# Ending the first attention layer in a block of its own, beside the next layers' loads and context products

## What is computed

```python
x = x + tanh(g_xattn[0]) * L0_xattn(layernorm(x), ctx)          # 16 heads of 32, context of 128 tokens
x = x + tanh(g_ffn[0])   * L0_ffn(layernorm(x))                 # 256 chosen tokens of each batch
x = x + tanh(g_xattn[1]) * L1_xattn(layernorm(x), ctx)          # 16 heads of 64
x = x + tanh(g_ffn[1])   * L1_ffn(layernorm(x))                 # ternary weights, conv
# L0_ffn:
scores = x @ w_router
_, idx = jax.lax.top_k(scores, 256)          # the tokens that are processed
x_sel = take(x, idx)                         # attention and gated MLP on them alone
out = x.at[idx].set(x_proc)
```

## Time and profile before

| | us |
|---|---|
| median of 3 runs | 1968.17 (1965.85 to 1969.87) |
| time of the profiled execution | 1974.4 |
| its span, first to last instruction | 1972.4 |
| attention slots (DVE's last L868 starts) | 482.06 |
| last gather issued | 536.67 |
| first load of the block that follows | 541.90 |
| first instruction of the second layer (L1812) | 578.83 |

### The profile page before, as it was taken

One profiled execution on the slowest core, in us unless ns is written; L12 is line 12 of the kernel. 1 busy time (PEld: TensorE's weight loads), 2 busy tenths in 40 slices (PEclk: granted clock), 3 DMA queues, 4 the chain that ended last, 5 costly groups with the idle time before them and its releaser, 6 DMA issues. The chain is left out here.

```text
span 1972.4 us, 24959 instructions
## 1 busy us (share of the span) xinstructions
PE 1615.3 (82%) x9331; PEld 934.4 (47%) x9331; DVE 1288.3 (65%) x2061; ACT 810.9 (41%) x1317; POOL 555.0 (28%) x482
## 2 busy tenths in 40 slices
PE   5788988887358879957899998999997267888886
PEld 3444444443143644424566665666664234444443
DVE  3468888888611442324477775777766379999996
ACT  3344444432012623223433432433432057777773
POOL 3222222211211200022221111102200077777771
PEclk9899999999679999977899999999998689999999
DMA  4012222012370233331101102012011230111211
GB/s 168 21 44 86 86 86 86 28 38 85 107 284 22 99 131 112 128 110 61 43 21 55 55 23 75 22 54 76 1 54 32 75 145 6 59 59 59 81 64 43
DMA packets 73124, 142.33 MB, mean 72 GB/s; under 512 B 8257, under 2 KB 17621, under 8 KB 72746
## 3 DMA queue, kind: packets, MB, share of 16 engines
q1 hardware_dynamic: 72042, 137.55, 19.6%
q0 software_dynamic: 960, 3.15, 0.5%
HBM read 97.67 MB, written 43.01 MB: 71 GB/s over the span
## 5 line engine op out<-in xcount | busy, mean ns | idle before, releaser
L2379 POOL TENSOR_TENSOR E_y<-E_y,E_centre 128x1024 f32<-128x1024 f32 x64 | 151.6, 2368 | 12.1 <-ACT E_y L2406 10.4
L2304 PE MATMUL E_OP<-E_w2q,E_yb 128*128 128x512 bf16 x512 | 130.6, 414 | 26.0 <-ACT E_yb L2391 21.7
L2295 PE MATMUL E_HP<-E_xT,E_w1q 128*128 128x512 bf16 x512 | 124.2, 387 | 8.9 <-DMA E_w1q<-w1b_d 6.1
L1232 ACT ACTIVATE D_oT<-D_OB 128x512 fp32r<-128x512 f32 x64 | 38.3, 599 | 224.9 <-DVE D_OB L1578 224.9
L2371 POOL TENSOR_SCALAR E_centre<-E_hs,E_cw,E_cb 128x512 f32<-128x512 f32 x64 | 107.9, 1686 | 63.6 <-DVE E_hs L2451 63.3
L1543 DVE TENSOR_TENSOR D_q_low<-D_PJ,D_q_high 128x512 fp32r<-128x512 f32 x62 | 42.9, 691 | 118.9 <-ACT D_q_high L1208 118.9
L1310 PE MATMUL D_PJ<-D_xT_high,D_wq_high 128*128 128x512 f32 x248 | 106.8, 431 | 9.2 <-DVE D_wq_low L1550 7.2
L2460 DVE SCALAR_TENSOR_TENSOR E_y<-E_hs,E_cw,E_y 128x512 f32<-128x512 f32 x128 | 107.1, 876 | 0.0
L592 PE MATMUL A_TX<-A_wo,A_oT 128*128 128x512 f32 x192 | 103.8, 670 | 0.7 <-DVE A_res L764 0.7
L1310 PE MATMUL D_PJ<-D_xT_high,D_wq_low 128*128 128x512 f32 x248 | 100.3, 404 | 0.0
L1310 PE MATMUL D_PJ<-D_xT_low,D_wq_high 128*128 128x512 f32 x248 | 99.7, 402 | 0.0
(11 more groups left out here) (341 smaller groups left out, 3992.9 us busy)
## 6 DMA issues: line engine op xcount, KB each, us to landing
A_x<-in_x SPq DMA_DIRECT2D x8, 1024.0 KB, 5.6
A_res<-in_x SPq DMA_DIRECT2D x8, 1024.0 KB, 5.6
x_d<-A_res SPq DMA_DIRECT2D x8, 1024.0 KB, 4.4
xn_d<-A_xn SPq DMA_DIRECT2D x8, 1024.0 KB, 6.4
W_raw<-in_w1T SPq DMA_DIRECT2D x16, 512.0 KB, 4.6
W_raw<-in_w2T SPq DMA_DIRECT2D x16, 512.0 KB, 4.2
D_x<-x_d SPq DMA_DIRECT2D x8, 1024.0 KB, 5.7
D_res<-x_d SPq DMA_DIRECT2D x8, 1024.0 KB, 5.8
```

The costliest lines, as they stand in the source:

```text
L2295: mm = pe.matmul(HP[:, i % 2, e, :], w1q[:, k, m * P:(m + 1) * P], XT[n % 2][:, k, :], start=k == 0, stop=k == KD - 1)
L2304: mm = pe.matmul(OP[:, :], yb[:, k, c * P:(c + 1) * P], w2q[:, k, :], start=k == 0, stop=k == MC - 1)
L2379: pool.tensor_tensor(y, y, U[i % 2][:, :, :], ALU.add).then_inc(t0, 1)
```

## The change

- The slots after the 32nd are taken out of the first block. A second block (`finish`) holds them, and in it SP loads the third layer's context weights and the second layer's first weights, PE makes the key and value tiles between the turned rows and sums (`tiles`: key tiles 0 to 2 in slot 36, 3 in 37, 4 and 5 in 38, 6 to 8 in 39, value tiles in 40), in three spare PSUM banks, ACT keeps them, and DVE makes the low part of the keys.
- `route` runs five slots behind for every chunk; `compare` six, `sum_lower` seven. Batch 0 is chosen two slots earlier (23 to 26), and its gather stands in POOL's list in step 7, j = 1.
- For chunks 26, 28 and 30 ACT makes the marks, by two activations, instead of DVE.
- The bias additions on POOL move from j = 0 and 1 to j = 2 and 3. A step's store waits for its normalised rows first; the residual of step n is loaded after the store of step n - 2.
- `project_out` of the last step has a bank for each chunk. A turned row waits for the score, not for the gated sum.
- Two weights of the second layer (W1, W2) are loaded from the second layer's first block.

```diff
-        block = ctx.enter_context(nc.Block())
+        OUT, ROUTE, ROW, SUMS = 4, 5, 6, 7
+        def by_act(q):
+            return q >= NB * NC - 6 and q % 2 == 0
+            def out_bank(n, c):
+                return (TXF, PJ[:, :], OB[:, :], ZB[:, :])[c] if n == STEPS - 1 else PJ[:, :] if c == SUB - 1 else TXF
+        def compare_by_act(act, s):
+
+            q = chunk_at(s, ROW)
+            if q is not None and by_act(q):
+                b, cc = divmod(q, NC)
+                w, k = (cc + 1) * P, acts_until(q)
+                act.wait_ge(row_kept, q + 1)
+                need(act, lower_act, k - 1)
+                act.activation(above[:, 0:w], s_row[b][:, 0:w], ACT.Relu, bias=own[:, q:q + 1], scale=-1.0)\
+                   .then_inc(above_ok, 1)
+                act.wait_ge(above_ok, k)
+                need(act, sum_mm, sums_done(q - 2))
+                act.activation(lower[q % 2][:, 0:w], above[:, 0:w], ACT.Sign, accum_out=less[:, q:q + 1])\
+                   .then_inc(lower_act, 1)
...
+        block = main.enter_context(nc.Block())
...
             for n in range(STEPS):
-                need(sp, stored[n % 2], 32 * (n // 2))
+                if n > 1:
+                    store(sp, n - 2)
+                    sp.wait_ge(stored[n % 2], 32 * (n // 2))
                 sp.dma_start(R[n % 2][:, :, :], x_dr[n // LAPS, n % LAPS]).then_inc(r_in[n % 2], 16)
...
-                    if c < 2:
-                        if c == 0:
+                    if c >= 2:
+                        if c == 2:
                             pool.wait_ge(r_in[n % 2], 16 * (n // 2 + 1))
-                        for i in (2 * c, 2 * c + 1):
+                        for i in (2 * c - 4, 2 * c - 3):
                             pool.tensor_tensor(R[n % 2][:, i, :], R[n % 2][:, i, :], bo[:, :], ALU.add)\
                                 .then_inc(biased, 1)
-            for c in range(SUB):
-                post_rstd(STEPS - 1, c)
-            for b in range(NB):
-                gather(b)
+                    if n == STEPS - 1 and c == 1:
+                        gather(pool, 0)
...
-                if n:
-                    add_out(n - 1, j)
-                    if j:
-                        route(n - 1, j - 1)
+                add_out(dve, s)
+                route(dve, s)
...
-                if n and j == GROUPS - 1:
-                    route(n - 1, SUB - 1)
-                compare(s)
-                choose(s)
+                compare(dve, s)
+                choose(dve, s)
+        main.close()
+        def finish(stage, prefetch):
+
+            tiles = {SLOTS + 4: range(0, 3), SLOTS + 5: range(3, 4), SLOTS + 6: range(4, 6), SLOTS + 7: range(6, 9),
+                     SLOTS + 8: range(9, stage.MT + stage.NV)}
+            with nc.Block() as block:
+                @block.sync
+                def _(sp):
+                    stage.load(sp)
+                    prefetch(sp)
+                    for n in (STEPS - 2, STEPS - 1):
+                        store(sp, n)
+                    for par in range(2):
+                        sp.wait_ge(stored[par], 32 * LAPS)
+
+                @block.gpsimd
+                def _(pool):
+                    for c in range(SUB):
+                        post_rstd(pool, STEPS - 1, c)
+                    gather(pool, 1)
+                    pool.wait_ge(chosen["got"], 16 * 2 * NB * HALVES)
+
+                @block.scalar
+                def _(act):
+                    for s in range(SLOTS, VIRTUAL):
+                        keep_row(act, s)
+                        keep_sums(act, s)
+                        compare_by_act(act, s)
+                        keep_found(act, s)
+                        for i in tiles.get(s, ()):
+                            if i < stage.MT:
+                                stage.keep_k(act, [i])
+                            else:
+                                stage.keep_v(act, [i - stage.MT])
+                            if i == stage.MT - 1:
+                                stage.high_k(act)
+
+                @block.tensor
+                def _(pe):
+                    for s in range(SLOTS, VIRTUAL):
+                        c = s - SLOTS
+                        if c < SUB:
+                            if c < 2:
+                                pe.wait_ge(fin, SUB * (STEPS - 2) + 3 + c)
+                            project_out(pe, STEPS - 1, c, 0, 1)
+                        turn_row(pe, s)
+                        find_tokens(pe, s)
+                        if s in tiles:
+                            pe.wait_ge(fin, SUB * (STEPS - 1) + 2)
+                            stage.multiply(pe, tiles[s])
+                        sum_lower(pe, s)
+
+                @block.vector
+                def _(dve):
+                    for s in range(SLOTS, VIRTUAL):
+                        add_out(dve, s)
+                        route(dve, s)
+                        compare(dve, s)
+                        choose(dve, s)
+                    stage.low_k(dve)
+
-def prepare_choice(nc, io, prefetch, context, chosen):
```

More of the change, by code:

```diff
@@ new lines, in sum_lower @@
+        def sum_lower(pe, s):
+            q = summed_at(s)
+            if q is not None:
+                if by_act(q):
+                    pe.wait_ge(lower_act, acts_until(q))
+                else:
+                    pe.wait_ge(lower_dve, q + 1 - acts_until(q))
+                pe.wait_ge(one_ok, 1)
+                need(pe, sum_kept, sums_done(q) - 1)
+                for i in range(q % NC):
+                    mm = pe.matmul(sum_ps[:, i:i + 1], lower[q % 2][:, i * P:(i + 1) * P], one[:, :], start=True, stop=True)
+                mm.then_inc(sum_mm, 1)
@@ new lines, in compare @@
+        def compare(dve, s):
+            q = chunk_at(s, ROW)
+            if q is None:
+                return
+            b, cc = divmod(q, NC)
+            w = (cc + 1) * P
+            dve.wait_ge(row_kept, q + 1)
+            need(dve, tied, q)
+            dve.scalar_tensor_tensor(out=ties_at[:, :], in0=s_row[b][:, cc * P:w], scalar=own[:, q:q + 1],
+                                     in1=following[:, :], op0=ALU.is_equal, op1=ALU.mult,
+                                     accum_out=ties[:, q:q + 1]).then_inc(tied, 1)
+            if not by_act(q):
+                if q >= 2:
+                    need(dve, sum_mm, sums_done(q - 2))
+                dve.tensor_scalar(lower[q % 2][:, 0:w], s_row[b][:, 0:w], own[:, q:q + 1], None, ALU.is_lt, ALU.add,
+                                  accum_out=less[:, q:q + 1]).then_inc(lower_dve, 1)
@@ L400, in _ @@
                     load_x(n + 3)
-                if n:
-                    store(n - 1)
-            store(STEPS - 1)
-            for par in range(2):
-                sp.wait_ge(stored[par], 32 * LAPS)
         @block.gpsimd
@@ L1842, in choice_layer, with _ @@
         with nc.Block() as block:
+            @block.sync
+            def _(sp):
+                for w, n in ((w1, "W1T"), (w2, "W2T")):
+                    sp.dma_start(w[:, :, :], io[n].rearrange("(k p) n -> p k n", p=P)).then_inc(later_in, 16)
             @block.vector
```

446 lines of the change are left out of this document (200 added, 246 removed).

## The result

The changed kernel took 1949.79 us (median of 7 runs, 1945.57 to 1956.54), beside 1969.72 for the kernel before (7 runs, 1965.85 to 1977.46): a ratio of 0.9897, 95% interval 0.987 to 0.9924, so 1.0% faster. The forecast was 1949.2, with a range of 1940 to 1960. The second layer starts at 555.50 in the profiled execution, 23.3 earlier than at 578.83; from there to the end it is 1394.3 us, 1395.6 before. All of the gain lies ahead of that point.

The account below looks back on a forecast made before the run. DVE-bound and PE-bound stretches stood one behind the other between slots and second layer. Its start, 549.4 + 8.5 = 557.9 against 578.83, gave -20.9, less 2 given back: -19, so 1949.2 us, range 1940 to 1960.

Parts of the forecast that it names:

- The order that costs: New block, slots 36 on: row 31 kept behind key tiles and ACT's chunk 30 marks; DVE waits 5 us to compare.
- The accumulated sign: ACT's marking passes over chunk 30: each 1.8 us, with bounds 1.8 and 3 because no trace showed it.
- last at 541.5, landed 3.6 later: End of the new block: last gather landed at 545.1, then 4.3 us of semaphore clearing before the second layer at 549.4.
- Four gathers are issued 1.25 apart: End of the new block, on POOL: after indices at 537.6, four evenly spaced gathers, the last at 541.5.
- The 2 us given back for key tiles at half speed: Slot 36 on PE: 2 us taken off the gain, up to 3.9 if all three key tiles are slow.
- the new block serves its products first: Rival: key-tile waits hold up marks, rows and sums; 1953 to 1960 us; chance 0.2, late stores included.
- M: What the attention slots gain or lose: +8.5 us, bounds +2 and +15.
- +2.7: j = 0 slots: DVE's `route` and wider compare ahead of L789 exceed its idle time, 2.7 us lost.
- -2: Choosing batch 0 two slots earlier puts its work into slot 23, where DVE idles: 2 us won.
- Cheaper meetings: Rival: L756 isn't blocked or the additions slip out of phase; M about +3, time about 1943; chance 0.2.
- Loads ahead of stores: Rival: new block's 7.9 MB of loads delays stores the last gather needs; 1949 to 1955; in the products-first rival's 0.2.
- Slower than before: Rival: additions meet DVE in j = 2 and 3, and gaps halve PE's clock; M = +44, decisive from 31; chance 0.03.

Follow-up runs that it names:

- project_two: Changed kernel with the last step's projections of chunks 28 and 29 at the end of PE's list in the first block: 1945.48 us, ratio 0.9861.
- marks_on_dve: Changed kernel with chunk 30 marked by DVE again instead of ACT: 1950.61 us, ratio 0.9895 to the kernel before.
- all_four: Changed kernel with the edits of additions_after_ties, project_two, marks_on_dve and low_k_after_issue together: 1932.03 us, ratio 0.9799.
- low_k_last: all_four with the semaphore for DVE's low part of the keys raised by a POOL memset behind the four gathers: 1932.27 us, ratio 0.9803.
- additions_after_ties: Changed kernel with each pair of POOL's bias additions held until DVE has counted the ties of the same slot: 1939.17 us, ratio 0.9841.
- project_first: Changed kernel with all four of the last step's projections at the end of PE's list in the first block: 1949.76 us, ratio 0.9883.
- all_route: all_four with the `route` of each token tile's fourth chunk back in j = 3: 1935.10 us, ratio 0.9801.
- additions_alone: Kernel before with only POOL's bias additions moved to j = 2 and 3: 1983.68 us, ratio 1.0053.
- low_k_after_issue: Changed kernel with DVE's low part of the keys waiting for a semaphore listed behind POOL's first gather: 1956.05 us, ratio 0.9908.

## Why the prediction was right, step by step

The time and its sign came out, and so did the shape of the sum. That the time came out to within 0.6 us is luck: several terms were off by 2 us and more, in both directions.

**The cut.** Counted from the end of the slots, in us (forecast, then measured): DVE's part of the first block ends 9.6, 9.6; PE's first product 10.4, 10.1; DVE's first `add_out` 16.2, 16.2; sums of 29 kept 38.6, 37.8; chunk 30 marked by ACT 42.4, 41.7; row 31 kept 44.0, 42.7; marks of 31 46.9, 45.3; indices 55.5, 55.6. The order that costs was read rightly from the two lists, and project_two and marks_on_dve show its price: each undid one link, and 6.3 and 4.3 went. One link was sized wrongly. The forecast had PE's sum of chunk 31 1.2 behind its marks. It ended 3.2 behind them, since key tile 3 had come late and slow, and the 1.6 won up to the marks were gone by the indices. The boundary, taken at 0.8, was 0.3 to 0.5 here. The accumulated sign cost 1.80 and 0.19 for its reading, at the lower bound.

**The landing and the clearing.** The step "last at 541.5, landed 3.6 later" and then "4.3 us as before" counted one thing twice. The 4.3 in rows 2 and 1 runs from the end of POOL's last gather to the next load, so the landing lay within it: the last gather of before landed at 540.39, 1.5 ahead of that load. Measured from the last gather's start to the second layer: 5.4, where I had 7.9. That is 2.5 too much.

**The gathers.** "Four gathers are issued 1.25 apart" missed the meeting of the first with the low part of the keys: 1.85 more. all_four and low_k_last show it, for the slow gather moved with L236 and went with it. The same paragraph placed the low part ("ends by 540") within 3 us of the gathers and didn't ask what one does to the other.

**The 2 us given back for key tiles at half speed.** About right in size and wrong in place. In after's trace tiles 0 to 2 take 1.46 to 1.48 each, but tile 3 took 2.78 and tile 4 1.80, some 1.6 in all, ahead of the sum of 31. The forecast's reason against it, that PE waits little from slot 37 on, failed: it waited 4.18 there. In additions_after_ties, project_first and all_route two of tiles 0 to 2 took 2.77 as well. The rival "the new block serves its products first" is this.

**M.** Forecast +8.5: additions +9.65, new order -1.2. Measured +6.6 against the profiled execution of before, and +9.5 without its odd interval. The sum is near; the division behind it can't be confirmed, because there is no single one. With the order taken first it is +4.5 and then +5.0 for the additions, with the additions first +13.1 and then -3.6. The forecast's parts lie between. Each of these four rests on single profiles, which can be 3 us apart, but the two divisions differ by 8.1. Adding the parts was the step that doesn't hold: what an addition costs depends on what stands in j = 3.

For the additions the meetings in j = 2 were foreseen in full: L783 by 1.0, and the first L756 by 1.0, in every step. The terms add up to 16 for the new ones; in j = 3 of steps 1 to 5 the forecast counted none, and there L535 is longer by 1.0 each, which makes 21. The slots end only 10.7 later for it, so about half was taken up by idle time, where the forecast took every meeting as lost (the old ones: 6.35 by its terms, 6.3 in the trace, 5.7 at the end of the slots). In j = 3 this can be seen: ahead of the low part of the queries DVE idles for 3.12, 2.80 and 2.17 us in slots 7, 11 and 15 of after, and for 4.17, 3.77 and 3.31 without additions. In additions_alone, where the second `route` is met, that idle time falls from 2.47, 2.12 and 2.46 to 0.37, 0 and 0.64.

For the order, without additions, "+2.7" in j = 0 measured 0.2, 0.6, 1.3, 0.8 and 1.7 into slots 13 to 29, 4.7 in all; and "-2" for choosing batch 0 earlier brought little on balance (the interval into slot 23 is 1.7 shorter, that into 24 1.3 longer). The "-1.9" for step 6 is there, into slot 28.

**The rivals.** Cheaper meetings: true in the new order, where they cost 5.0 of 9.65, and not in the old, where they cost 13.1; and not for the reason given, since L756 is blocked. Loads ahead of stores: the issue of step 6's second store took 8.76 us behind them (next fence), and the last of step 7's began at 526.75, 17.7 ahead of the first gather; hidden, as said. Slower than before: additions_alone shows that its mechanism is real, 13.1 us in the slots and 0.5% in the time, in the order of before; far from the 31 that it needed. SP's stores in the new block of after:

```profile
508.67 8.76 SPq L393 DMA_DIRECT2D x_d<-A_res  x1
...
526.75 0.38 SPq L393 DMA_DIRECT2D x_d<-A_res  x1
```

The sum: +6.6 for 8.5, and 66.9 for 69.3 between, so -23.3 for -19. The profiled execution of before was 4.7 above its median, and has the odd interval of 3.0 in it. Without that the second layer's start moved by 20.4, and the medians moved by 19.9, beside a forecast of 19: the total fitted better than its terms.

## What to carry to other kernels

When a long wait of one stage is laid under another stage's work, the gain is what the profile promises, but what is left of it is decided by the order of the lists at the seam: here 6.3 us for a projection that stood behind the cut and 4.3 for marks on ACT that held up the emptying of PE's banks, and with it a key tile that stood ahead of the last sum. Ask of every instruction in front of the late one whether it had to be there. An operation of a spare engine that slows the bound one by sharing its memory access needs no new slot, only a wait that puts it behind the instruction it meets: 8 to 11.5 us of the slots here, about half of what the whole change won. And costs of two moves that touch the same list are not to be added: here the same additions cost 18.8 us in one order and 10.7 in the other. And an estimate whose two halves overlap (a landing, then a gap that contains it) is found by asking where each row begins and ends.

## What the runs showed of the hardware

- A gather on POOL can be held up for the whole of a VectorE instruction with two SBUF inputs. In each of the ten traces in which a gather met L236 it took 2.78 to 3.00 us instead of 0.94 to 1.00, and it ended 0.8 to 0.9 after L236 did, so nearly the whole gather came behind it; in low_k_last, where none met it, none was slow. A short meeting costs less: batch 0's first gather in after (471.07, 1.33 us) overlapped L524 (0.75, two SBUF inputs) and its neighbours and was 0.4 longer. The Trainium skill (SBUF — State Buffer, "SBUF: two separate sides") describes the trap for an instruction in a two-port mode, which keeps GpSimd from writing descriptors until it ends; this case shows it for a `tensor_tensor` of 2048 columns in 2.29 us, with two SBUF inputs, which that section counts only against a GpSimd operation that reads SBUF.
- POOL's additions beside DVE's work on SBUF lengthened both: L524 in j = 2 from 0.75 to between 1.75 and 1.78, the first L861 (f32, one SBUF input) to 1.50 from 0.54, L535 to 1.37 from 0.34, and POOL's own 128x512 addition to 1.6 to 1.7 from 1.3.
- A semaphore that POOL's sequencer raises behind the gathers in its list says nothing of their execution: it fell before the first gather in low_k_after_issue and after the first in all_four. Raised by a memset behind them, it came at the end of the fourth.
- A boundary between two blocks, without clearing, costs 0.3 us from the last engine's end to SP's first load and 0.5 to PE's first product where DVE or PE ended last (after, project_first, project_two); where POOL's additions ended last (additions_after_ties) it was 0.65 and 0.85.
- PE's pauses come back as half speed: after 8.04 us of waiting the projection of chunk 28 took 6.1 (granted clock 0.50 for its first 3.8 us), in project_two, without the pause, 3.60 (granted clock 1.00). After 4.18 us of waiting key tile 3 took 2.78 (0.53), in marks_on_dve, after 0.47, 1.53 (1.00).
